# Two-layer transformer and RWKV block: VectorE copies for the first attentions, PE-repeated values for the last two sequences, another PSUM bank for the last recurrence, and a new order

## What is computed

```
# layer 0, per sequence
q, k, v = split(layernorm(x) @ w_qkv + b_qkv)                 # 16 heads of 16
x = x + attention(q, k, v, ltor_mask) @ w_ao + b_ao           # "self", a = 0
x = x + attention(layernorm(x) @ w_q, kv(encoder_states), cross_mask) @ w_co + b_co   # "cross", a = 1
x = x + gelu(layernorm(x) @ w1 + b1) @ w2 + b2
# attention: softmax(q k' / 4 * mask - 10000 (1 - mask)) v
# layer 1, per sequence (token shift: previous token minus this one)
xn = ln(x); sx = shift(xn)
x5 = xn + sx * (maa_stack + tanh((xn + sx * maa_x) @ maa_w1) @ maa_w2)      # five mixed streams
w = exp(-exp(time_decay + tanh(x5[1] @ decay_w1) @ decay_w2))
r, k, v, g = x5[3] @ Wr', x5[0] @ Wk', x5[2] @ Wv', silu(x5[4] @ Wg')
for each token, 32 heads with a state s of 8 x 8:
    out = r . (u * k v' + s);  s = k v' + w * s
x = x + (groupnorm(out) * gn_w + gn_b) * g @ Wo'
x = x + sigmoid(xr @ ffn_Wr') * (relu(xk @ ffn_Wk')^2 @ ffn_Wv')
```

## Time and profile before

| | us |
|---|---|
| median of 3 runs | 699.7 (697.33 to 701.93) |
| the profiled execution | 699.4, its span 697.3 |
| PE busy | 644.4 (92%) |
| DVE busy | 587.9 (84%) |
| ACT busy | 575.3 (83%) |
| POOL busy | 322.8 (46%) |
| mean granted TensorE clock | 0.983 |

### The profile page before, as it was taken

How to read it: one execution, slowest core, us unless ns; L and a number is a source line. 1 busy time by engine, 2 the same in 40 slices (tenths; PEclk the granted TensorE clock), 3 DMA queues, 4 the chain that set the end, 5 groups by cost and what they waited for, 6 DMA issues and landing times.

```text
span 697.3 us, 17053 instructions
## 1 busy us (share of the span) xinstructions
PE 644.4 (92%) x5763; PEld 559.7 (80%) x5763; DVE 587.9 (84%) x1420; ACT 575.3 (83%) x2083; POOL 322.8 (46%) x441
## 2 busy tenths in 40 slices
PE   6787999999999999999999999999999989797765
PEld 5566888898889898989889898889898868676654
DVE  2576579999999999999999999999999997858562
ACT  2689999899999999999999999999999986752311
POOL 1154362646455465636363746455465544324111
PEclk9999999999999999999999999999999999899999
DMA  8920032222323050505031222323040505050500
GB/s 302 325 70 9 1 86 53 75 64 62 85 55 92 15 131 2 144 2 136 11 104 43 76 70 62 85 56 90 16 130 2 144 2 136 2 132 6 136 8 8
DMA packets 54843, 52.77 MB, mean 76 GB/s; under 512 B 6126, under 2 KB 49510, under 8 KB 54374
## 3 DMA queue, kind: packets, MB, share of 16 engines
q1 hardware_dynamic: 54758, 51.70, 26.8%
HBM read 30.72 MB, written 4.19 MB: 50 GB/s over the span
## 4 chain that ended last, share of the span: by engine, by line
PE 74%; ACT 8%; DVE 8%; issue 4%; DMA 3%; POOL 2%; SPq 0%; POOLq 0%; DVEq 0%; ACTq 0%
PE PS_B L503 15%; PE PS_S L503 7%; PE PS_T L597 6%; PE PS_B L637 6%; PE PS_D L510 5%; PE PS_S L578 4%; PE PS_T L605 4%; PE PS_S L510 4%; PE PS_T L510 4%; ACT SC L1130 3%; PE PS_D L727 2%; PE PS_B L646 2%; DMA V<-values_by_head 2%; PE PS_B L659 2%; PE PS_D L503 2%
## 5 line engine op out<-in xcount | busy, mean ns | idle before, releaser
L1130 ACT ACTIVATE SC<-SC,NMX 128x128 f32<-128x128 f32 x512 | 200.6, 402 | 5.7 <-DVE NMX L876 5.4
L1130 ACT ACTIVATION_READ_ACCUMULATOR SC<-SC,NMX 128x1 f32 x512 | 103.1, 201 | 0.0
L876 DVE TENSOR_REDUCE NMX<-SC 128x4 f32<-128x512 f32 x128 | 84.5, 673 | 2.4 <-POOL SC L1299 1.7
L597 PE MATMUL PS_T<-CST,SC 128*128 128x128 f32 x512 | 78.7, 277 | 7.2 <-ACT PT L1138 3.0
L1138 ACT ACTIVATE PT<-PS_T 128x512 f32<-128x512 f32 x128 | 76.3, 596 | 9.6 <-PE PS_T L597 9.1
L597 PEld LDWEIGHTS PS_T<-CST,SC 128*128 128x128 f32 x512 | 60.1, 141 | 19.3 <-ACT SC L1130 7.8
L1341 POOL TENSOR_TENSOR SS<-SS,KR 128x1024 f32<-128x1024 f32 x16 | 37.8, 2363 | 76.8 <-DVE SS L948 76.8
L948 DVE TENSOR_TENSOR_SCAN SS<-W,AJ 128x1024 f32<-128x1024 f32 x32 | 73.1, 2284 | 0.0
L1299 POOL TENSOR_TENSOR SC<-SC,MADD 128x512 f32<-128x512 f32 x48 | 61.3, 1280 | 22.5 <-DVE SC L851 21.5
L1301 POOL TENSOR_TENSOR SC<-SC,MADD 128x512 f32<-128x512 f32 x32 | 40.7, 1272 | 59.9 <-DVE SC L851 59.9
L503 PE MATMUL PS_B<-MX,W 128*128 128x128 f32 x512 | 66.2, 278 | 0.8 <-ACT KR L1185 0.8
(11 more groups left out here) (161 smaller groups left out, 1589.5 us busy)
## 6 DMA issues: line engine op xcount, KB each, us to landing
W<-EW SPq DMA_DIRECT2D x32, 512.0 KB, 4.8
V<-values_by_head SPq DMA_DIRECT2D x32, 512.0 KB, 5.7
W<-in_weights SPq DMA_DIRECT2D x1, 4160.0 KB, 21.0
ENC<-in_enc SPq DMA_DIRECT2D x16, 128.0 KB, 2.4
values_by_head<-VC SPq DMA_DIRECT2D x16, 128.0 KB, 1.8
out<-X SPq DMA_DIRECT2D x16, 128.0 KB, 5.9
X<-in_x SPq DMA_DIRECT2D x1, 1920.0 KB, 15.9
W<-in_weights SPq DMA_DIRECT2D x1, 1280.0 KB, 8.6
```

The lines of the kernel that those rows point to most:

```text
L597: last = pe.transpose(PS_T[:, j * T:(j + 1) * T], SC[:, nr(b, a) % 2, g, j, :], ident)
L876: dve.tensor_reduce(NMX[:, nr(b, a) % 2, GH * g:GH * g + GH], SC[:, nr(b, a) % 2, g], AX_X, ALU.max, negate=True)\
L1130: last = act.activation(SC[:, nr(b, a) % 2, g, j, :], SC[:, nr(b, a) % 2, g, j, :], ACT.Exp, bias=NMX[:, nr(b, a) % 2, h:h + 1], accum_out ...
```

## The change

1. `FIRST = 4`: for attentions 0 to 3, DVE copies the turned probabilities of groups 1 and 3 (eight copies of 128 x 512), and ACT those of groups 0 and 2. A helper `copied` makes PE wait for the right counts.
2. `LAST = 2`: for sequences 14 and 15 the store to DRAM and the two loads fall away. PE repeats the values by 8 products for each half (`b_select`, with a 0/1 matrix `SEL` that POOL makes at the start) into `PS_S`, which the attentions no longer use, and `d_outer` reads `PS_S`. For these two, `d_rstate` of half 1 is done by DVE and no longer by POOL.
3. `dbank(b)`: the recurrence of sequence 15 uses `PS_T` and no longer `PS_D`, with GM, GV and GY. Its `d_own` waits for the last attention (`a_res`) and not for `d_f` of sequence 14. Some new waits guard tiles that sequences 14 and 15 share. Extra products of the identity write to other banks.
4. All tables but SP's are in a new order.

```diff
+LAST = 2
+FIRST = 4
...
+        def dbank(b):
+            return PS_D if b < B - 1 else PS_T
...
+        def copied(pe, n, g):
+            by_dve = 2 * min(n, FIRST) + ((g + 1) // 2 if n < FIRST else 0)
+            pe.wait_ge(a_pt, 4 * n + g + 1 - by_dve)
+            if n < FIRST and g:
+                pe.wait_ge(a_dpt, by_dve)
...
             def warm(name, arg, b):
                 n = KEEP_WARM[(name, arg, b)] if (name, arg, b) in KEEP_WARM else 0
-                if n and b > 2:
-                    pe.wait_ge(a_masked, 8 * B)
+                bank = PS_B[:, 0, :]
+                if n and b > 2 and name[0] == "d" and b == B - 1:
+                    pe.wait_ge(b_v, B)
+                    pe.wait_ge(b_g, B)
+                elif n and b > 2:
+                    bank = PS_T
+                    pe.wait_ge(a_res, 2 * B)
...
+            def b_select(b, t):
+                if b >= B - LAST:
+                    pe.wait_ge(set_sel, 1)
+                    pe.wait_ge(b_v, b + 1)
+                    pe.wait_ge(d_a, 2 * b - 1 + t if b > B - LAST else 0)
+                    for g in (2 * t, 2 * t + 1):
+                        scores_read(pe, 2 * B - 1, g)
+                    for d in range(RS):
+                        last = pe.matmul(PS_S[:, 2 * t + d // GH, d % GH, :], SEL[:, d, :], VC[:, t, :],
+                                         start=True, stop=True)
+                    last.then_inc(b_v8ps, 1)
...
-                pe.wait_ge(d_f, b)
+                if b < B - 1:
+                    pe.wait_ge(d_f, b)
+                else:
+                    pe.wait_ge(a_res, 2 * B)
...
+            def a_prob_copy(b, arg):
+                a, g = arg
+                if nr(b, a) < FIRST:
+                    dve.wait_ge(a_turned, 4 * nr(b, a) + g + 1)
+                    dve.tensor_copy(PT[:, g], PS_T[:, :].rearrange("p (j n) -> p j n", n=T)).then_inc(a_dpt, 1)
...
-                    dve.wait_ge(b_v8, 32 * b + 32)
+                    dve.wait_ge(b_v8, 32 * min(b + 1, B - LAST))
+                v = V8[:, t]
+                if b >= B - LAST:
+                    dve.wait_ge(b_v8ps, 2 * (b - B + LAST) + t + 1)
+                    v = PS_S[:, 2 * t:2 * t + 2].rearrange("p g j n -> p (g j) n")
...
-    ("a_out", 1, 3), ("a_key", 1, 2), ("b_valgate", 0, 4), ("b_valgate", 1, 4), ("d_yturn", 0, 5), ("a_query", 1, 2),
+    ("b_select", 0, 4), ("b_turn", 0, 3), ("d_out", 0, 5), ("a_prob_turn", (0, 2), 1), ("b_mlp1", 0, 3),
```

More of the change, by code:

```diff
@@ L85 @@
 PE_ORDER = [
-    ("a_scores", 0, 1), ("a_prob_turn", (1, 1), 3), ("d_own", 0, 5), ("b_low2", 2, 4), ("a_prob_turn", (1, 2), 3),
-    ("d_read", 0, 5), ("b_decay1", 0, 4), ("a_prob_turn", (1, 3), 3), ("d_oturn", 0, 5), ("b_decay2", 0, 4),
-    ("b_keyrec", 0, 4), ("a_enc_turn", 0, 2), ("a_pv", 1, 3), ("a_val", 1, 2), ("a_turn", 1, 2), ("b_keyrec", 1, 4),
-    ("a_out", 1, 3), ("a_key", 1, 2), ("b_valgate", 0, 4), ("b_valgate", 1, 4), ("d_yturn", 0, 5), ("a_query", 1, 2),
-    ("a_prob_turn", (0, 0), 1), ("a_scores", 1, 2), ("b_turn", 0, 3), ("d_out", 0, 5), ("a_prob_turn", (0, 1), 1),
@@ new lines @@
+    ("a_prob_turn", (1, 2), 3), ("b_decay1", 0, 4), ("d_oturn", 0, 5), ("a_prob_turn", (1, 3), 3),
+    ("b_decay2", 0, 4), ("b_keyrec", 0, 4), ("a_enc_turn", 0, 2), ("b_keyrec", 1, 4), ("a_pv", 1, 3),
+    ("a_val", 1, 2), ("b_valgate", 0, 4), ("a_turn", 1, 2), ("b_valgate", 1, 4), ("a_key", 1, 2), ("a_out", 1, 3),
+    ("d_yturn", 0, 5), ("a_query", 1, 2), ("a_prob_turn", (0, 0), 1), ("a_scores", 1, 2), ("a_prob_turn", (0, 1), 1),
+    ("b_select", 0, 4), ("b_turn", 0, 3), ("d_out", 0, 5), ("a_prob_turn", (0, 2), 1), ("b_mlp1", 0, 3),
@@ L594, in a_prob_turn @@
                 else:
-                    pe.wait_ge(a_pt, 4 * nr(b, a) + g)
+                    copied(pe, nr(b, a), g - 1)
                 for j in range(GH):
@@ L600, in a_pv @@
             def a_pv(b, a):
-                pe.wait_ge(a_pt, 4 * nr(b, a) + 4)
+                copied(pe, nr(b, a), 3)
                 for t in range(CT):
@@ L1136, in a_prob_copy @@
                 a, g = arg
+                if g % 2 and nr(b, a) < FIRST:
+                    return
                 act.wait_ge(a_turned, 4 * nr(b, a) + g + 1)
@@ L1237, in d_affine @@
                 for t in range(CT):
[L1238 removed]
+                    last = act.activation(dbank(b)[:, C + t * T:C + (t + 1) * T], dbank(b)[:, t * T:(t + 1) * T], ACT.Identity,
                                           bias=GNC[:, 1, t:t + 1], scale=GNC[:, 0, t:t + 1])
```

203 lines of the change are left out of this document (114 added, 89 removed).

## The result

The changed kernel takes 706.14 us (median of 8 runs, 702.74 to 710.58), the kernel before 700.11 us on the same chip: a ratio of 1.0086, with an interval of 1.0054 to 1.0118. It is slower, where 0.6% faster was forecast, and lies 3.1 us above the range. The profiled execution took 707.9 us, its span is 706.1 (before 699.4 and 697.3).

What follows compares the result with a forecast made beforehand. PE was taken to bound the middle, with gains only at start and end, whose chains run through ACT and the values' DRAM round trip. Terms -1.2 + 0.8 - 1.5 + 0 - 2.2 = -4.1 gave 695.6 us, range 689 to 703.

Steps and rivals of the forecast that it cites:

- What bounds the kernel: Whole kernel: PE has no idle time in the middle, so an order can only lose there; gains come from start and end.
- Part 1, the start: Start: eight copies moved to DVE and the new order together bring -1.2 us, range -2.4 to +1.0.
- The term for the copies: Start: relieving ACT of five copies on its chain, 0.48 us each, can bring at most 2.4 us; half was taken.
- the walk of the new order: Start, turn 2: following the new lists puts the cross attention's query and scores about 1.0 us later; ACT recovers by turn 3.
- Part 2, the middle: Full turns: PE waits 0.07 us per turn between `b_turn` 1 and `b_low1`, +0.8 us over 11 turns; bounds 0 to +9.2.
- rival C: Middle: the new order loses 0.3 us per turn, 3.3 us in all, giving 698.1 us; chance 0.12.
- VectorE's extra pairs: Middle: two more pairs where a DVE instruction waits for the one just ahead, at about 0.13 us each.
- Part 3, turn 17: Turn 17: the XK product cuts PE's 3.21 us pause and the clock stays full, -1.5 us; bounds 0 to -2.85.
- Part 4, the last two sequences: End: PE repeating values instead of DRAM brings 0 for sequence 14 (1.8 either way), -2.2 us for sequence 15.
- 27 us as now: End: a sign to check, that `d_read` of sequence 15 starts about 27 us before the end, unchanged.
- D: Middle: ACT reaches `b_scale` 1 late by a whole exponential group, 1.6 us per turn, giving 712.4 us; chance 0.11.
- no change: Whole kernel: a time between 692.7 and 706.7 us, about 1% or 7 us either way; chance 0.55.

Runs made afterwards that it cites:

- the five slow ones: Five of 8 traces of kernels with the old order in turn 17, whose turn 17 took 37.53 to 37.74 us at clock 0.91.
- second trace: The kernel before, run once more unchanged: 698.95 us, a single execution.
- The four corners: From turn 15's end: old order 165.0 us (values through DRAM), 167.1 (by PE); new order from turn 17, 168.1 and 161.9, seam's 2.15 off the 168.1.

## Why the prediction was wrong, step by step

**What bounds the kernel.** Right, and it should have carried more weight: an order can only lose in the middle. But the sentence that gains can come from the start did not ask what the new order can lose there.

**Part 1, the start (-1.2, range to +1.0; it was +6.1).** This step failed. The term for the copies has the right sign (0.3 to 4 us gained with the new lists). What has no row behind it is the half that I took of its 2.4 us. What failed is the walk of the new order: I put the delay of the query and the scores at 1.0 us and let ACT make up for it by turn 3. I named that values and keys now stand behind `a_pv` and gave it no price. Measured, the scores of sequence 1 come 24.4 us after the first in place of 19.7, and nothing makes up for it. PE's list alone costs 8.1 us by turn 3, ACT's alone 3.9. The upper bound was the error: here a piece that left a gap cost its length, the idle time that it left (2.24 us ahead of one turn of probabilities), and the clock of what followed (0.50 between 25 and 35 us).

**Part 2, the middle (+0.8; it was +5.2 in ten turns, with +1.5 in turns 4 and 5).** The step priced one place, `b_turn` 1 to `b_low1`, at 0.07 us per turn. PE has no wait for XX there in the middle; this place is right. The failed step is "I looked for the place where PE must wait": there were three others (HG 0.21, the query 0.14, B_LT 0.10), where an input comes just too late. In part this is the place on PE: B_LT starts 1.54 us after the turn of its rows (451.88 - 450.34), before 1.80. It is not so for the query, where one turn of probabilities stands between in both lists; there VectorE's result comes later. ACT's slower instructions are an open part of it. Of rival C's size, 0.3 a turn, the loss is 1.7 times; its cause, VectorE's extra pairs, is not what the runs show for the half that was tried.

**Part 3, turn 17 (-1.5; it was -2.5 there and +0.8 in turn 16).** Right in its mechanism. The trace shows the pause cut in two and the clock full:

```profile
611.00 1.16 PE L540 MATMUL PS_D<-XK,W 128*128 128x128 f32 x8 [1.49 <-DVE XK L1114]
612.51 0.44 PE L533 MATMUL PS_B<-CST,B_N 128*128 128x128 f32 x2 [0.35 <-DVE B_N L870]
...
615.89 1.16 PE L683 MATMUL PS_B<-XX,W 128*128 128x128 f32 x8 [1.64 <-DVE XX L973]
```

The kernel before kept its clock there in its second trace and had 1.56 us without any change, so the size depends on the trace that one compares with: 0.95 us against this one, 2.4 to 2.6 against the five slow ones. The table above shows that the cut pause mostly keeps the clock. The gain is thus real and on average larger than the 1.5 reckoned; that it stood on one trace was a risk that the step didn't name.

**Part 4, the last two sequences (0 and -2.2; it was +0.7 and -2.9).** Right in size and in the path, but not in what it made of the clock. ACT, PE and VectorE in the changed kernel:

```profile
662.91 0.38 ACT L1270 ACTIVATE VC<-PS_B 128x256 f32<-128x256 f32 x1 [2.21 <-PE PS_B L540]
663.39 2.02 PE L747 MATMUL PS_S<-VC,SEL 128*128 128x128 f32 x16
669.81 1.97 PE L747 MATMUL PS_S<-VC,SEL 128*128 128x128 f32 x16
674.74 1.06 PE L540 MATMUL PS_D<-XK,W 128*128 128x128 f32 x8
680.91 1.06 PE L779 MATMUL PS_T<-SS,CST 128*32 128x512 f32 x8 [0.50 <-DVE CV L1030]
678.96 0.42 DVE L1121 SCALAR_TENSOR_TENSOR RR<-RR,PS_D 128x256 f32<-128x256 f32 x1 [1.11 <-PE PS_D L547]
```

From the copy's end (663.29) to `d_read` it takes 17.6 us; 18.4 was forecast, 20.6 it was. `b_select` takes 2.02 and 1.97, the product with XK 1.06 at full clock in place of 2.07, from it to the mixing 4.22 (4.32 forecast), and `d_read` to the end 25.2 (25; the "27 us as now" among the signs was a slip, the kernel before has 25.0). The step laid the 6.05 us from that product to the mixing on its half speed. The second trace of the kernel before has the product at full speed and the same 6.05 us (667.66 - 661.61):

```profile
661.61 1.16 PE L503 MATMUL PS_D<-XK,W 128*128 128x128 f32 x8 [2.64 <-DVE XK L1049]
665.46 2.28 DVE L948 TENSOR_TENSOR_SCAN SS<-W,AJ 128x1024 f32<-128x1024 f32 x1
667.66 0.40 DVE L1056 SCALAR_TENSOR_TENSOR RR<-RR,PS_D 128x256 f32<-128x256 f32 x1
```

Before, the mixing stands behind VectorE's second scan, and the clock cost nothing there. In the changed kernel the values come earlier, one scan fewer stands in that stretch, and VectorE waits 1.11 us for PE: that is where the 4.22 comes from. So the forecast of 4.32, taken from the last sequence, was right for another reason than the clock. Also, the step took the repeated values as the cause and the order as given. The four corners show that in the old order they bring nothing.

**The rivals and their chances.** D, the slower one, had the wrong mechanism (ACT late to `b_scale` 1 by a whole group) and 0.11; the result is slower for two reasons that no rival had. By the forecast's own lines (692.7 and 706.7) the result still falls under "no change", with 0.55; those lines were wider than the measurement, whose interval is 1.0054 to 1.0118. The fault is the same in both: I wrote four edits as four terms and searched each for what it brings, while the fourth, the new order, touched every turn.

## What to carry to other kernels

- A new order of all lists is the largest edit of a change, though it adds no work. Price it in each stage by itself, and most in the one that fills the pipeline: list for each piece that moved which gap it leaves.
- In a stage where an engine is 99% busy, compare the distance of starts of its pieces in both traces, not the waits: 0.45 of the 0.52 us a turn was found as pieces of 0.1 to 0.2. Compare the mean durations of the other engines' instructions too.
- Lists of several engines belong together. Here two lists each cost the start by themselves, undoing PE's gave nothing back, and two edits that each lose alone gain together. Undo one, do one alone, and do both before a cause is named; and take the gain where it is: the old order for the start and the middle, the new one for the end, was the best version.
